# Rotary halves swapped by DMA instead of a second projection, and the second layer's gates on GpSimd

## The chip, the cores and the metric

One core of a Trainium2 chip runs one program. The time is device microseconds of the whole program, median of the runs. The engines named below are TensorE (PE: PE for matmuls, PEld for weight loads), VectorE (DVE), ScalarE (ACT), GpSimd (POOL) and SyncE (SP), which here only issues DMAs. Each engine runs its own instructions strictly in the order in which they are written and waits at semaphores, so an instruction that waits holds up everything behind it on its engine.

## What is computed

Two transformer layers over x of shape (8, 512, 128). What the change touches is the first attention, with 16 query heads and 4 key heads of 64, and the gates of the second attention. For each of them the reference says:

```python
def _rotate_half(t):
    t1, t2 = (t[..., :DH // 2], t[..., DH // 2:])
    return jnp.concatenate([-t2, t1], axis=-1)
...
q = q * cos + _rotate_half(q) * sin
k = k * cos + _rotate_half(k) * sin
...
attn = jax.nn.softmax(attn, axis=-1)
...
g = jax.nn.sigmoid(g.reshape(B, H, T, 2, 4).sum(-1))
gate_a = g[..., 0:1]
gate_b = g[..., 1:2]
gate_a_1 = gate_a * (gate_b * grep_a - 1.0) + 2.0
attn = attn + gate_a_1 * position_bias[None]
probs = jax.nn.softmax(attn, axis=-1)
```

The middle line on softmax belongs to the first attention, the last lines to the second one. After each attention comes a small feed-forward part, which the change leaves alone.

## The kernel before

**The first attention** works on 64 pairs of heads (8 sequences of 8 pairs), one pair to a *step*. The function `pipeline` writes the order of one step as eight *slots* by hand, and all engines walk through the same list, each taking its own part. Steps 3 to 50 are three rounds of a loop of 16 steps; the others are written out. In step s the list has:

- `C` (s, i), one in each slot: two 512-column matmuls give the scores of one key tile (L446, L448), ScalarE exponentiates them (L516), and `L` takes the rounding rest of the exponentials, on VectorE for two of the eight tiles (L607) and on GpSimd for six (L664).
- `D`: probabilities times values, eight blocks of twelve short matmuls (L464 to L466); VectorE normalises after each half (L613, L615). The first block of a half needs all `L` tiles of that half.
- `A` for pair s+3: the query projection, in three 512-column matmuls for q and three more for q with the halves of each head exchanged (L409 to L411; the exchanged weights are a copy made at the start, L559). VectorE multiplies both by cosine and sine in one pass into `rcs` (L585).
- `RS`, `RH`, `RL` for the same pair: GpSimd adds the two products (`rot`, L647), ScalarE rounds to 16 bits (`rhi`, L522), GpSimd takes the rest (`rlo`, L652). At `RL` SyncE waits for `rlo` and issues four DMAs that lay hi and lo parts out as query rows (L364, L366).
- `B` for pair s+2, four times: scores of the rounded parts for the row maximum (L431), reduced by VectorE (L600). `MX` and `M` turn the maxima, and SyncE sends them with one small DMA (L381) that `C` of the next step waits for.
- `O`: the transposes of a finished pair (L473, L538).

Once in eight steps come `W` (the output projection, L479, with L623 and L669), `HT` (transposes of the normalised input, L401), `K` twice (like `A`, for keys, with six DMAs each at `KL`, L375 to L377) and `V`. `A`, `K`, `B`, `M`, `O`, `V`, `HT` and `W` are *jobs*: each takes one of two PSUM buffers `ps_m`, which it can fill when the reader of the job before the last has freed it.

**The second attention** does its score products partly on VectorE and partly on GpSimd, in four rounds (`for r in range(QT)`). In a round VectorE makes the gates (L1440, L1443, L1446) with a drain behind each, then four products and eight sums, then the `residual` of the round before (L1431), which waits for TensorE, and only then the scores (L1464 to L1469); ScalarE exponentiates, and both engines multiply by the values (`p_prod`, L1477 and L1392). GpSimd multiplies the gates into the bias after its own score products (L1384). `statistics` and `spread` are the layer norm of a later round.

## Time and profile before

| what | value |
|---|---|
| median of 3 runs | 1565.05 us (1561.4 to 1566.12) |
| profiled execution, time | 1566.98 us |
| profiled execution, span of its instructions | 1565.2 us |
| first attention, first to last exponential | 93.9 to 863.7 us |
| second attention with its weights | about 1125 to 1337 us |
| TensorE busy, whole span | 1159.0 us |

A timeline row gives the start in us from the span's start, the duration in us, engine, line, operation, output and inputs, shape and count, and in square brackets how long the engine stood idle before it and who released it. A matmul's duration overlaps the next one's, so what one costs is read from the distance between starts.

### The profile page before, as it was taken

To read this page: it belongs to the slowest core of one execution; us is meant where nothing else is said; L and a number is where in the kernel's file an instruction comes from. 1 tells how busy PE (TensorE), PEld (TensorE's weight loads), DVE (VectorE), ACT (ScalarE), POOL (GpSimd) and SP (SyncE) were. 2 spreads that over 40 slices of the span, in tenths; PEclk is the share of its full clock that TensorE was granted. 3 is DMA by queue.
4 is the path that set the end of the run, shared out by engine and by line. 5 is a ranking of instruction groups with operands and counts; after the bars stand their busy time and mean duration, and the time that the engine had idled before them with its cause. 6 is when DMAs were issued, how large, how long until landed. Compare 5 with 4: busy or idle time off the path is not lost. (4 is left out here: it accounts for less than half of the span.)

```text
span 1565.2 us, 29826 instructions
## 1 busy us (share of the span) xinstructions
PE 1159.0 (74%) x10864; PEld 749.5 (48%) x10864; DVE 1129.2 (72%) x1571; ACT 608.1 (39%) x1176; POOL 835.0 (53%) x754
## 2 busy tenths in 40 slices
PE   2288999989999899999999446555358776165554
PEld 1135565646656556566666324434126566133343
DVE  2477978768788587787878368984339786568983
ACT  1135545445455364554546123332133330133331
POOL 0267879778788687887878123231035453023320
PEclk9589999999999999999999768987656788668986
DMA  2322113122132121311211000000000000000001
GB/s 65 87 45 59 39 32 66 43 49 51 33 66 43 29 60 32 66 43 37 61 34 31 15 0 1 1 0 0 24 1 1 1 0 1 14 1 0 1 0 54
DMA packets 52197, 46.37 MB, mean 30 GB/s; under 512 B 7734, under 2 KB 50250, under 8 KB 52042
## 3 DMA queue, kind: packets, MB, share of 16 engines
q1 hardware_dynamic: 52042, 44.33, 12.6%
q8 instruction: 94, 1.54, 0.4%
q14 instruction: 61, 0.50, 0.1%
HBM read 6.42 MB, written 2.10 MB: 5 GB/s over the span
## 5 line engine op out<-in xcount | busy, mean ns | idle before, releaser
L664 POOL TENSOR_TENSOR a_p_lo<-a_probs 128x512 f16<-128x512 f32 x384 | 419.8, 1115 | 26.2 <-ACT a_probs L516 22.7
L516 ACT ACTIVATE a_probs<-a_ps_s 128x512 f32<-128x512 f32 x512 | 303.6, 596 | 328.6 <-PE a_ps_s L448 321.1
L600 DVE TENSOR_REDUCE a_nmx<-a_ps_m 128x2 f32<-128x1024 f32 x256 | 311.1, 1216 | 39.3 <-PE a_ps_m L431 37.6
L464 PE MATMUL a_ps_o<-a_v_hi,a_probs 128*128 128x65 f16 x2048 | 238.7, 194 | 7.0 <-POOL a_p_lo L664 7.0
L466 PE MATMUL a_ps_o<-a_v_hi,a_p_lo 128*128 128x65 f16 x2048 | 238.0, 194 | 0.0
L465 PE MATMUL a_ps_o<-a_v_lo,a_probs 128*128 128x64 f16 x2048 | 237.8, 193 | 0.0
L464 PEld LDWEIGHTS a_ps_o<-a_v_hi,a_probs 128*128 128x128 bf16 x2048 | 191.5, 98 | 61.6 <-issue 14.6
L465 PEld LDWEIGHTS a_ps_o<-a_v_lo,a_probs 128*128 128x128 bf16 x2048 | 189.3, 98 | 44.1 <-issue 0.6
L446 PE MATMUL a_ps_s<-a_qq,a_kk 128*128 128x512 f16 x512 | 195.8, 382 | 10.6 <-issue 6.5
L448 PE MATMUL a_ps_s<-a_qq,a_k_l 65*128 65x512 f16 x512 | 196.7, 384 | 0.0
L825 PE MATMUL f_ps_gu<-f_w_gu,f_hqT 128*128 128x352 f32 x256 | 122.9, 643 | 90.5 <-DVE f_h L912 79.5
L466 PEld LDWEIGHTS a_ps_o<-a_v_hi,a_p_lo 128*128 128x128 f16 x2048 | 189.1, 97 | 0.0
L431 PE MATMUL a_ps_m<-a_kk,a_rhi 128*128 128x512 f16 x512 | 155.8, 386 | 16.4 <-DMA a_k_l<-a_rlo 9.5
L585 DVE TENSOR_TENSOR a_rcs<-a_ps_m,a_cossin 128x1024 f32<-128x1024 f32 x80 | 98.0, 1225 | 65.5 <-PE a_ps_m L411 64.7
L607 DVE TENSOR_TENSOR a_p_lo<-a_probs 128x512 f16<-128x512 f32 x128 | 143.2, 1119 | 1.7 <-ACT a_probs L516 1.7
L825 PEld LDWEIGHTS f_ps_gu<-f_w_gu,f_hqT 128*128 128x128 f32 x256 | 65.1, 267 | 140.2 <-issue 115.8
L647 POOL TENSOR_TENSOR a_rot<-a_rcs 128x512 f32<-128x512 f32 x80 | 107.8, 1347 | 45.3 <-DVE a_rcs L585 45.2
L652 POOL TENSOR_TENSOR a_rlo<-a_rot,a_rhi 128x512 f16<-128x512 f32 x80 | 92.6, 1157 | 40.1 <-ACT a_rhi L522 40.1
L998 POOL TENSOR_TENSOR f_q<-f_r,f_s 128x512 f32<-128x512 f32 x16 | 16.9, 1057 | 139.6 <-DVE f_r L932 139.6
L1287 PE MATMUL a_ps_o<-a_p_prod,ident 128*128 128x128 f32 x512 | 68.6, 304 | 28.7 <-DVE a_p_prod L1477 28.7
L431 PEld LDWEIGHTS a_ps_m<-a_kk,a_rhi 128*128 128x128 f16 x512 | 43.4, 99 | 93.0 <-DVE a_nmx L600 39.2
L848 PE MATMUL f_ps_y<-f_w_dn,f_h2T 128*128 128x128 f32 (+1 forms) x384 | 56.4, 301 | 36.4 <-ACT f_h2T L889 36.4
(217 smaller groups left out, 2123.5 us busy)
## 6 DMA issues: line engine op xcount, KB each, us to landing
a_qq<-a_rhi SPq DMA_DIRECT2D x128, 128.0 KB, 2.4
a_kk<-a_rhi SPq DMA_DIRECT2D x64, 128.0 KB, 2.4
a_qq<-a_rlo SPq DMA_DIRECT2D x128, 64.0 KB, 2.1
a_k_l<-a_rlo SPq DMA_DIRECT2D x32, 64.0 KB, 2.1
out_x<-x_sb SPq DMA_DIRECT2D x1, 2048.0 KB, 8.7
a_qq<-a_nmT SPq DMA_DIRECT2D x64, 2.0 KB
m_w<-in_wmod SPq DMA_DIRECT2D x2, 384.0 KB
a_probs<-in_wq SPq DMA_DIRECT2D x1, 512.0 KB, 3.5
```

Source lines behind the costliest of these rows:

```text
L431: last = nc.tensor.matmul(ps_m[:, n % 2, k, :], rhi[:, r % NR, qt * 128:(qt + 1) * 128], kk[:, b % 2, 2 * j // G0, 1 + h, :], start=True, ...
L446: nc.tensor.matmul(ps_s[:, i % 2, :], kk[:, b % 2, g, 0, kt * 128:(kt + 1) * 128], q_hl[:, p % 4, h, :], start=True, stop=False)
L448: nc.tensor.matmul(ps_s[:, i % 2, :], k_l1[:, b % 2, g, kt * 128:(kt + 1) * 128], q_hm[:, p % 4, h, :], start=False, stop=True).then_inc(s ...
L464: nc.tensor.matmul(out, hi, v_hi[:, b % 2, kt, g, 0:65], start=(kt == 0), stop=False)
L465: nc.tensor.matmul(out[:, 0:DH0], hi, v_lo[:, b % 2, kt, g, :], start=False, stop=False)
L466: last = nc.tensor.matmul(out, lo, v_hi[:, b % 2, kt, g, 0:65], start=False, stop=(kt == QT - 1))
L516: nc.scalar.activation(probs[:, p % 2, kt, h, :], ps_s[:, i % 2, :], ACT.Exp, scale=DH0 ** -0.5).then_inc(exp_done, 1)
L600: nc.vector.tensor_reduce(nmx[:, p % 2, 2 * i:2 * i + 2], ps_m[:, n % 2, :, :], axis=X, op=ALU.max, negate=True).then_inc(free[n % 2], 1)
L607: nc.vector.tensor_tensor(p_lo[:, p % 2, kt, h, :], pr, pr.bitcast(BF16)[:, 1:2 * L:2], ALU.subtract).then_inc(lo_dve, 1)
L647: nc.gpsimd.tensor_tensor(rot[:, r % 2, :], rcs[:, r % 2, 0, :], rcs[:, r % 2, 1, :], ALU.add).then_inc(rope_sum, 1)
L664: nc.gpsimd.tensor_tensor(p_lo[:, p % 2, kt, h, :], pr, pr.bitcast(BF16)[:, 1:2 * L:2], ALU.subtract).then_inc(lo_pool, 1)
L825: last = nc.tensor.matmul(ps_gu[:, t, a, 0:INNER], hqT[:, (2 * half + t) * 128:(2 * half + t + 1) * 128], w_gu[:, a * INNER:(a + 1) * INNE ...
```

## The change

In the first attention the second half of each projection goes: `A` and `K` are three matmuls into one bank, and the exchanged weights, their copies and a drain at the start go too. VectorE multiplies the one bank by cosine and by sine in the same single instruction (it reads the bank twice by a broadcast). The sine product is then moved by 32 partitions: a new item (`RD`, `KD`) on SyncE waits for VectorE and issues four DMAs of 32 partitions by 2 KB each into `rsw`, and the sum on GpSimd waits for these four. The slots are written anew: `A` comes first in its step, `B` in slots 1, 3, 5, 7, `O` in slot 2, and the sum, the rounding and the rest in slots 4, 5 and 6; for keys they reach into the next step. VectorE takes `L` tiles 3 and 7 instead of 2 and 6.

In the second attention the gates move to GpSimd, as four instructions with a drain behind each, behind its score products. On VectorE the residual of the round before now comes after the scores.

```diff
@@ pipeline
+        if pair(s + 3):
+            slots[0].append(("A", s + 3))
+            slots[1].append(("RD", s + 3))
+            slots[4].append(("RS", s + 3))
+            slots[5].append(("RH", s + 3))
+            slots[6].append(("RL", s + 3))
         if pair(s + 2):
             for i in range(4):
-                slots[2 * i].append(("B", s + 2, i))
-        if pair(s + 3):
-            slots[1].append(("A", s + 3))
-            slots[3].append(("RS", s + 3))
-            slots[4].append(("RH", s + 3))
-            slots[5].append(("RL", s + 3))
+                slots[2 * i + 1].append(("B", s + 2, i))
...
         if pair(s - 2):
-            slots[3].append(("O", s - 2))
+            slots[2].append(("O", s - 2))
...
         if (b := seq(-5)) is not None:
             for m in range(2):
-                slots[2 + 3 * m].append(("K", b, m))
-                slots[4 + 2 * m].append(("KS", b, m))
-                slots[5 + 2 * m].append(("KH", b, m))
-                slots[6 + m].append(("KL", b, m))
+                slots[2 + 2 * m].append(("K", b, m))
+                slots[3 + 2 * m].append(("KD", b, m))
+                slots[5 + 2 * m].append(("KS", b, m))
+            slots[6].append(("KH", b, 0))
+            slots[7].insert(0, ("KL", b, 0))
         if (b := seq(-4)) is not None:
+            slots[0].append(("KH", b, 1))
+            slots[1].append(("KL", b, 1))
...
-        LO_DVE, LO_POOL = (2, 6), (0, 1, 3, 4, 5, 7)
+        LO_DVE, LO_POOL = (3, 7), (0, 1, 2, 4, 5, 6)
@@ sync
+                if kind in ("RD", "KD"):
+                    key = it[1:]
+                    r = rope[key]
+                    t.jobs(free, job[("A" if kind == "RD" else "K",) + key], 1)
+                    for k in range(4):
+                        src, dst = slice(32 * k, 32 * (k + 1)), slice(32 * (k ^ 1), 32 * (k ^ 1) + 32)
+                        sp.dma_start(rsw[dst, r % 2, :], rcs[src, r % 2, 1, :]).then_inc(rope_swap[r % 2], 16)
@@ tensor
-                    for swap in range(2):
-                        out = ps_m[:, n % 2, swap, :]
-                        hi, lo = (w[:, swap, j * 128:(j + 1) * 128] for w in (w_hi, w_lo))
-                        nc.tensor.matmul(out, hi, hT_hi[:, b % 2, :], start=True, stop=False)
-                        nc.tensor.matmul(out, hi, hT_lo[:, b % 2, :], start=False, stop=False)
-                        last = nc.tensor.matmul(out, lo, hT_hi[:, b % 2, :], start=False, stop=True)
+                    hi, lo = (w[:, j * 128:(j + 1) * 128] for w in (w_hi, w_lo))
+                    nc.tensor.matmul(bank, hi, hT_hi[:, b % 2, :], start=True, stop=False)
+                    nc.tensor.matmul(bank, hi, hT_lo[:, b % 2, :], start=False, stop=False)
+                    last = nc.tensor.matmul(bank, lo, hT_hi[:, b % 2, :], start=False, stop=True)
@@ vector, before the loop
-            for w, heads in ((wq_hi, H0), (wq_lo, H0), (wk_hi, KV0), (wk_lo, KV0)):
-                w4 = w[:].rearrange("p s (h a c) -> p s h a c", h=heads, a=2)
-                for a in range(2):
-                    last = nc.vector.tensor_copy(w4[:, 1, :, a, :], w4[:, 0, :, 1 - a, :])
...
-                    nc.vector.tensor_tensor(rcs[:, r % 2, :, :], ps_m[:, n % 2, :, :], cossin[:],
+                    nc.vector.tensor_tensor(rcs[:, r % 2, :, :], ps_m[:, n % 2, 0:1, :].to_broadcast([128, 2, L]), cossin[:],
                                             ALU.mult).then_inc(free[n % 2], 1)
@@ gpsimd
-                    t.jobs(free, job[("A" if kind == "RS" else "K",) + key], 1)
+                    t.wait(rope_swap[r % 2], (r // 2 + 1) * 64, ROPE16 // 2 * 64)
                     t.ropes(rope_lo, r - 1, 1)
-                    nc.gpsimd.tensor_tensor(rot[:, r % 2, :], rcs[:, r % 2, 0, :], rcs[:, r % 2, 1, :],
+                    nc.gpsimd.tensor_tensor(rot[:, r % 2, :], rcs[:, r % 2, 0, :], rsw[:, r % 2, :],
                                             ALU.add).then_inc(rope_sum, 1)
@@ second attention, gpsimd
-                pool.wait_ge(gate_ok, r + 1)
+                pool.wait_ge(sig_ok, r + 1)
+                if r >= 1:
+                    pool.wait_ge(gbias_ok, r)
+                nc.gpsimd.tensor_tensor(gate[:], sig[:, r % 2, :, 1, :],
+                                        grep_a[:].unsqueeze(1).to_broadcast([128, B, H1]), ALU.mult)
+                nc.gpsimd.drain()
+                nc.gpsimd.tensor_tensor(gate[:], gate[:], gate_c[:, 0:1, :].to_broadcast([128, B, H1]), ALU.subtract)
+                nc.gpsimd.drain()
+                nc.gpsimd.tensor_tensor(gate[:], gate[:], sig[:, r % 2, :, 0, :], ALU.mult)
+                nc.gpsimd.drain()
+                nc.gpsimd.tensor_tensor(gate[:], gate[:], gate_c[:, 1:2, :].to_broadcast([128, B, H1]), ALU.add)
+                nc.gpsimd.drain()
+                if r >= 1:
+                    pool.wait_ge(score_ok, r)
@@ second attention, vector
-                dve.wait_ge(sig_ok, r + 1)
-                if r >= 1:
-                    dve.wait_ge(gbias_ok, r)
-                nc.vector.tensor_tensor(gate[:], sig[:, r % 2, :, 1, :],
...
-                nc.vector.tensor_scalar(gate[:], gate[:], 2.0, None, ALU.add).then_inc(gate_ok, 1)
...
-                if has(r - 1):
-                    residual(r - 1)
                 dve.wait_ge(gbias_ok, r + 1)
...
                                         ALU.subtract).then_inc(score_ok, 1)
+                if has(r - 1):
+                    residual(r - 1)
```

SyncE in one ordinary step inside the loop and at the start of the next, before. The first four rows are the query rows of one pair, `a_qq<-a_nmT` is the turned maxima:

```order
80 L364 DMA a_qq<-a_rhi 64x2x512 [waits a0_rlo]
81 L366 DMA a_qq<-a_rlo 64x512
82 L364 DMA a_qq<-a_rhi 64x2x512
83 L366 DMA a_qq<-a_rlo 64x512
84 L292 REGISTER_ALU
85 L381 DMA a_qq<-a_nmT 1x8x128 [waits a0_free0]
```

The same place after, from one pair's swap to the next pair's:

```order
163 L370 DMA a_rsw<-a_rcs 32x512 [waits a0_free1]
164 L370 DMA a_rsw<-a_rcs 32x512 x3
165 L298 REGISTER_ALU
166 L394 DMA a_qq<-a_nmT 1x8x128 [waits a0_free1]
167 L298 REGISTER_ALU
168 L377 DMA a_qq<-a_rhi 64x2x512 [waits a0_rlo]
169 L379 DMA a_qq<-a_rlo 64x512
170 L377 DMA a_qq<-a_rhi 64x2x512
171 L379 DMA a_qq<-a_rlo 64x512
172 L298 REGISTER_ALU
173 L370 DMA a_rsw<-a_rcs 32x512 [waits a0_free1]
174 L370 DMA a_rsw<-a_rcs 32x512 x3
```

Four swap DMAs now stand ahead of the maxima, and the next pair's swap stands behind the four query DMAs, which wait for `rlo`.

GpSimd in the step with the keys, after (two steps' worth of sums, `a_rot`, and rests, `a_rlo`):

```order
188 L652 TENSOR_TENSOR a_rot<-a_rcs,a_rsw 128x512 [waits a0_rlo,a0_rswap0]
189 L298 REGISTER_ALU
190 L669 TENSOR_TENSOR a_p_lo<-a_probs 128x512 [waits a0_edone]
191 L652 TENSOR_TENSOR a_rot<-a_rcs,a_rsw 128x512 [waits a0_rlo,a0_rswap1]
192 L298 REGISTER_ALU
193 L657 TENSOR_TENSOR a_rlo<-a_rot,a_rhi 128x512 [waits a0_rhi]
194 L298 REGISTER_ALU
195 L669 TENSOR_TENSOR a_p_lo<-a_probs 128x512 [waits a0_edone]
```

Each sum waits for a swap (`a0_rswap`), where before it waited for VectorE alone, and the query's `rlo` stands behind the first key's sum.

VectorE in the second attention, from the sums of a round to its scores, before (`a1_psum`, `a1_full` are TensorE's):

```order
897 L1450 TENSOR_TENSOR a_s_prod<-a_ps_q,a_qkvg 128x1024
898 L1414 TENSOR_REDUCE a_score<-a_s_prod 128x128 [waits a1_smd] x2
899 L1414 TENSOR_REDUCE a_score<-a_s_prod 128x128 [waits a1_smp] x4
900 L1431 TENSOR_TENSOR x_sb<-a_ps_r,x_sb 128x4x128 [waits a1_full0]
901 L1431 TENSOR_TENSOR x_sb<-a_ps_r,x_sb 128x4x128 [waits a1_full1]
902 L1464 TENSOR_TENSOR a_score<-a_score,a_gbias 128x1024 [waits a1_ssum,a1_gbias]
```

and after:

```order
885 L1461 TENSOR_TENSOR a_s_prod<-a_ps_q,a_qkvg 128x1024
886 L1435 TENSOR_REDUCE a_score<-a_s_prod 128x128 [waits a1_smd] x2
887 L1435 TENSOR_REDUCE a_score<-a_s_prod 128x128 [waits a1_smp] x4
888 L1473 TENSOR_TENSOR a_score<-a_score,a_gbias 128x1024 [waits a1_ssum,a1_gbias]
889 L1476 TENSOR_REDUCE a_mx<-a_score 128x128
890 L1478 TENSOR_TENSOR a_score<-a_score,a_mx 128x1024
891 L1452 TENSOR_TENSOR x_sb<-a_ps_r,x_sb 128x4x128 [waits a1_full0]
```

The residual's two instructions have moved from ahead of the scores to behind them.

## Rows read from the trace of the kernel before

**Rows 1.** The page's first part: busy time, share of the span, instructions.

```profile
PE 1159.0 (74%) x10864; PEld 749.5 (48%) x10864; DVE 1129.2 (72%) x1571; ACT 608.1 (39%) x1176; POOL 835.0 (53%) x754
```

**Rows 2.** Busy time in stretches: eight steps, W's step, K's and V's, an ordinary one.

```profile
core 0: us, PE busy (x) PEld busy (x) DVE busy (x) ACT busy (x) POOL busy (x), PEclk, DMA share, GB/s
408.62:506.09 97.47, 94.15 (x1142) 59.61 (x1142) 78.22 (x105) 51.53 (x102) 80.34 (x73) 1.00 0.23 48
408.62:428.42 19.80, 18.08 (x200) 13.80 (x200) 12.02 (x18) 7.37 (x14) 12.11 (x12) 1.00 0.12 25
428.42:454.75 26.33, 24.73 (x287) 14.93 (x286) 19.65 (x24) 14.02 (x27) 23.66 (x22) 1.00 0.38 82
475.36:485.60 10.24, 10.24 (x133) 6.12 (x132) 9.07 (x12) 6.03 (x13) 8.92 (x9) 1.00 0.20 42
```

**Rows 3.** Timeline of the ordinary step 475.36 to 485.60, all engines.

```profile
476.31 0.38 PE L409 MATMUL a_ps_m<-a_hT_hi,a_wq_hi 128*128 128x512 f16 x1
...
477.39 0.38 PE L411 MATMUL a_ps_m<-a_hT_hi,a_wq_lo 128*128 128x512 f16 x1
...
477.90 1.23 DVE L585 TENSOR_TENSOR a_rcs<-a_ps_m,a_cossin 128x1024 f32<-128x1024 f32 x1 [0.95 <-PE a_ps_m L411]
...
479.20 1.27 POOL L647 TENSOR_TENSOR a_rot<-a_rcs 128x512 f32<-128x512 f32 x1 [0.50 <-DVE a_rcs L585]
...
480.51 1.04 POOL L664 TENSOR_TENSOR a_p_lo<-a_probs 128x512 f16<-128x512 f32 x1
...
481.64 0.62 ACT L522 ACTIVATE a_rhi<-a_rot 128x512 f16<-128x512 f32 x1
...
482.33 1.16 POOL L652 TENSOR_TENSOR a_rlo<-a_rot,a_rhi 128x512 f16<-128x512 f32 x1 [0.79 <-ACT a_rhi L522]
...
483.52 0.63 SPq L364 DMA_DIRECT2D a_qq<-a_rhi  x1
...
485.48 1.66 SPq L366 DMA_DIRECT2D a_qq<-a_rlo  x1
```

**Rows 4.** The page's costliest groups: VectorE's cosine and sine product.

```profile
L585 DVE TENSOR_TENSOR a_rcs<-a_ps_m,a_cossin 128x1024 f32<-128x1024 f32 x80 | 98.0, 1225 | 65.5 <-PE a_ps_m L411 64.7
```

**Rows 5.** DMA issues: KB each, median us from issue to landing.

```profile
a_qq<-a_rlo SPq DMA_DIRECT2D x128, 64.0 KB, 2.1
...
a_b_hl<-a_b_lo SPq DMA_DIRECT2D x1, 0.8 KB, 1.7
```

**Rows 6.** Timeline of TensorE, 406 to 448 us: W, and HT behind its wait.

```profile
408.35 7.31 PE L479 MATMUL a_ps_m<-a_wo,a_oT 128*128 128x128 f32 x64
...
424.01 0.65 PE L401 MATMUL a_ps_m<-ident,a_xhat 128*128 128x128 f32 x4 [1.50 <-DVE a_nmx L600]
```

**Rows 7.** Timeline of the start: first sum, first B; below, the first exponential.

```profile
63.88 1.27 POOL L647 TENSOR_TENSOR a_rot<-a_rcs 128x512 f32<-128x512 f32 x1 [4.14 <-DVE a_rcs L585]
...
76.53 1.01 PE L431 MATMUL a_ps_m<-a_kk,a_rhi 128*128 128x512 f16 x2 [9.45 <-DMA a_k_l<-a_rlo]
...
93.88 0.60 ACT L516 ACTIVATE a_probs<-a_ps_s 128x512 f32<-128x512 f32 x1 [3.01 <-PE a_ps_s L448]
```

**Rows 8.** Timeline of the second attention, round 1, all engines.

```profile
1201.60 1.49 DVE L1440 TENSOR_TENSOR a_gate<-a_sig,a_grep_a 128x128 f32<-128x128 f32 x1
...
1207.29 2.34 DVE L1450 TENSOR_TENSOR a_s_prod<-a_ps_q,a_qkvg 128x1024 f32<-128x1024 f32 x2
...
1214.21 2.34 POOL L1384 TENSOR_TENSOR a_gbias<-a_gate,a_bias 128x1024 f32<-128x1024 f32 x1
...
1228.91 0.69 DVE L1431 TENSOR_TENSOR x_sb<-a_ps_r,x_sb 128x512 f32<-128x512 f32 x1 [6.88 <-PE a_ps_r L1268]
...
1230.92 1.22 DVE L1464 TENSOR_TENSOR a_score<-a_score,a_gbias 128x1024 f32<-128x1024 f32 x1
...
1235.41 0.60 ACT L1351 ACTIVATE a_ps_p<-a_score 128x512 f32<-128x512 f32 x1 [4.18 <-DVE a_score L1469]
...
1237.56 4.58 DVE L1477 TENSOR_TENSOR a_p_prod<-a_ps_p,a_qkvg 128x1024 f32<-128x1024 f32 x4
```

More of the change, by code:

```diff
@@ L236, in layer0_attention @@
         rcs = sb("rcs", [128, 2, 2, L])
+        rsw = sb("rsw", [128, 2, L])
         rot = sb("rot", [128, 2, L])
@@ L488, in _ @@
             nc.scalar.activation(ident16[:], ident[:], ACT.Copy).then_inc(ready, 1)
-            for whole, hi in ((wq, wq_hi[:, 0, :]), (wk, wk_hi[:, 0, :]), (wv, wv_hi[:])):
+            for whole, hi in ((wq, wq_hi[:]), (wk, wk_hi[:]), (wv, wv_hi[:])):
                 nc.scalar.activation(hi, whole, ACT.Copy, scale=WSCALE).then_inc(w_hi_done, 1)
@@ L550, in _ @@
             dve.wait_ge(w_hi_done, 3)
-            for whole, hi, lo in ((wq, wq_hi[:, 0, :], wq_lo[:, 0, :]), (wk, wk_hi[:, 0, :], wk_lo[:, 0, :]),
-                                  (wv, wv_hi[:], wv_lo[:])):
-                nc.vector.scalar_tensor_tensor(out=lo, in0=whole, scalar=WSCALE, in1=hi, op0=ALU.mult,
-                                               op1=ALU.subtract)
-            nc.vector.drain()
-            for w, heads in ((wq_hi, H0), (wq_lo, H0), (wk_hi, KV0), (wk_lo, KV0)):
-                w4 = w[:].rearrange("p s (h a c) -> p s h a c", h=heads, a=2)
-                for a in range(2):
-                    last = nc.vector.tensor_copy(w4[:, 1, :, a, :], w4[:, 0, :, 1 - a, :])
-            last.then_inc(swapped, 1)
+            for whole, hi, lo in ((wq, wq_hi[:], wq_lo[:]), (wk, wk_hi[:], wk_lo[:]), (wv, wv_hi[:], wv_lo[:])):
+                last = nc.vector.scalar_tensor_tensor(out=lo, in0=whole, scalar=WSCALE, in1=hi, op0=ALU.mult,
+                                                      op1=ALU.subtract)
+            last.then_inc(split, 1)
             def item(t, it):
```

31 lines of the change are left out of this document (15 added, 16 removed).

## Prediction

> **What bounds the kernel now.** The busy shares of the whole span say little: TensorE is at 74% and VectorE at 72% [rows 1], averages over stages with different limits. So the first attention, half of the span, is read by its steps. A cycle of eight steps (one sequence) takes 97.47 us [rows 2]. An ordinary step takes 10.24 us and TensorE is busy for all of it, with 9.07 for VectorE and 8.92 for GpSimd [rows 2]. A busy TensorE need not be a full one, but in the timeline its matmuls of that step stand start to start with no idle bracket [rows 3]: it sets the 10.24. Two places are different. W's step takes 19.80, of which W is 7.31 and a wait of HT for VectorE's reduction 1.50 [rows 2, 6]. The step with K and the one with V take 26.33 together, 23.66 of it GpSimd's [rows 2]. In the second attention VectorE paces each round: it works on gates from 1201.60 to 1207.29, later stands idle for 6.88 us at the residual, and only then makes the scores that ScalarE waits 4.18 us for [rows 8].
>
> **What leaves TensorE.** Six projection matmuls start at 476.31 to 477.39, so one costs 1.08 / 5 = 0.216 us [rows 3]. Three go in each of 80 ropes [rows 4]: 0.65 us a step, 80 x 0.65 = 52 us in all. An ordinary step would need 10.24 - 0.65 = 9.59 us of TensorE. VectorE's product keeps its one pass of 1.23 us over as many elements; a broadcast read is not in the trace, I take it at the same price (if it cost twice, VectorE's 9.07 would rise to 10.3 and the gain would be gone). Its wait of 0.95 us for the projection [rows 3] only shrinks.
>
> **What takes its place on SyncE.** This decides the forecast. Before, the sum followed VectorE's product at once: `rot` starts at 479.20, right after the product of 477.90 + 1.23 [rows 3]. Now SyncE issues four DMAs first. Behind them on SyncE's queue stand the maxima and then the four query DMAs, and these wait for `rlo`, which comes out of this very swap; the next pair's swap stands behind them. So one turn around SyncE, DMA, GpSimd and SyncE can't overlap with the next one. Its length, from rows:
> - first to fourth swap issue: query DMAs go at 483.52 and, three issues later, 485.48, so 0.65 apiece: 1.96;
> - landing of the fourth: 2.1, as for the 64 KB `rlo` rows [rows 5]; between 1.7 (the 0.8 KB row) and 2.4 as the outer ends;
> - `rot` 1.27, the `p_lo` tile between it and `rlo` 1.04, `rlo` 1.16 [rows 3] (ScalarE's `rhi`, 0.62, hides beside the tile);
> - four query issues 2.6, and 0.2 for five handovers of some 0.04.
>
> Sum 1.96 + 2.1 + 3.47 + 2.6 + 0.2 = 10.3 us. That is more than TensorE's 9.59 and hardly less or more than today's 10.24: **SyncE's turn replaces TensorE as the bound, and an ordinary step keeps its time.** Some issues take longer, like the 1.66 at 485.48 [rows 3]; before they hid, now eight of eight stand in the turn. I take 10.55 a step, with 10.0 and 11.3 as ends (short landing; one long issue in each turn). The first two steps after V can borrow about 1 us, since a swap may lag behind its product by that much before TensorE feels it.
>
> **The eight-step cycle.** (a) W's 7.3 us give SyncE's turn all the slack it needs, so its step and the one before it cost TensorE's work: 30.04 before; after 2 x 9.59 + 7.31 + 0.44 for HT's transposes = 26.9. HT's 1.50 goes, since in the new order HT waits for a reduction two jobs back that is done by then. -2.9 with 0.2 of small waits. (b) K's and V's steps. I followed the queues from K's step's projection at 0: product ends 2.1, swap issued to 4.8, landed 6.3, `rot` to 7.5; the first key's product ends about 6.4 (behind the first reduction on VectorE), its swap lands 10.5, and GpSimd holds `rlo` of the query behind that sum: `rlo` 13.0. Then SyncE issues without a gap: 4 query DMAs to 15.6, 6 key DMAs to 19.6, the next swap to 22.2, 6 key DMAs to 26.1, and only then the maxima, landed 28. The scores of V's successor wait for those, so the pair of steps takes 28.5, against 26.33: +2.2, with long issues +2.6. TensorE would need some 22. (c) The other four steps: 9.6 + 10.2 + 2 x 10.55 = 40.9 against 41.1. Sum of a cycle: -2.9 + 2.6 - 0.2 = -0.5 us; seven cycles carry ropes: **-4 us** (ends: -35 and +30).
>
> **The start.** Eight weight copies and three matmuls ahead of the first product go, 1.3 us each. Then the first sum (63.88) waits for a swap, 1.96 + 2.1 + 0.4; the second key's and the first query's swap queue behind the first's and behind twelve key DMAs, so the first B (76.53) comes about 6 us later, and the first scores wait for maxima that stand behind one more swap: the first exponential (93.88) about 7.5 us later [rows 7]. **+7.5 us.**
>
> **The second attention.** Gates off VectorE: 1207.29 - 1201.60 = 5.7 us a round. GpSimd's four gate operations are 128 wide: its 1024-wide one takes 2.34 [rows 8], an eighth is 0.3, with a drain 0.45, so four take about 2 us; VectorE's own small ones took up to 2.2 each there, and four of those, 9 us, are the upper end. They stand behind GpSimd's score products, which end at 1214.2 [rows 8], and the scores need the bias from about 1221: 7 us of cover less 2.34. So they cost nothing at the lower price, and about 4 us a round at the upper one in the first round, less later, when GpSimd starts earlier.
> The residual is on the round's cycle: TensorE's sums, its turn through ScalarE, residual, then the 4.5 us of scores (1230.92 to the exponential at 1235.41) and the exponential, then `p_prod` at 1237.56. With scores first, they run inside the 6.88 us of idle time, and `p_prod` follows residual and statistics at once. What is late next is ScalarE (sigmoid and two table loads until about 1231). Round 1: -4.5 for the scores and -3 carried from round 0, whose GpSimd products no longer wait for `spread`; round 2 another -4; round 3 another -1, since there the residual hid almost entirely. **-12 us** (ends -6 and -13).
> Beside this, the rule of the Trainium skill, *GPSIMD Engine Reference*, Engine selection, that elementwise work with two inputs is about twice as slow on GpSimd as on VectorE, speaks against moving gates: at twice VectorE's undisturbed 0.7 us they would be 6 us, still within the cover of all rounds but the first.
>
> **Sum.** 1566.98 (the profiled execution) - 4 + 7.5 - 12 = 1558.5; it lay 1.9 us above the median, so **1556.5 us**.
>
> **Rivals.**
> *The turn is shorter than TensorE's step.* Landing at 1.7 and an issue of 0.5 would give 9.3. Then the 52 us come, less what GpSimd's lag costs (swap data reach it 6 us after the projection, and the next block of D waits for tiles behind it: about 9.75 a step). Cycle: 5 x -0.5, -2.4 for W's step, -2 for K and V: -7, seven times -49 with the start at +5 and -12: 1508; half of it 1530. Against it: every SBUF to SBUF issue in the rows takes 0.6 or more.
> *The turn is longer, and the kernel slower.* Place: SyncE's queue between the query DMAs and the next swap. The forecast's -8.5 is used up when an ordinary turn takes 0.25 us more than 10.55 (35 such steps), so from 10.8. With a long issue in each turn, or ScalarE's `rhi` stuck behind an exponential as in the 0.79 us wait before `rlo` [rows 3], it is 11.3: 35 x 0.75 = 26 more, and some 6 in K's and V's steps: 1588.
> *Gates late on GpSimd.* The upper price eats most of the second attention's gain: 1565.
> *The swap's form.* The Trainium skill, *DMA: Bandwidth & Descriptors*, Rules for kernel authors, says that transfers to disjoint partition parts serialise and should be one. Here the rows give the cost: 1.96 us of the turn are the three extra issues. By that rule one DMA would make the turn 8.4 us; the change has four, so it stays a reason for the bound, not a time of its own.
> That the change doesn't do what it says is out: TensorE's list has three matmuls a projection.
>
> **Chances.** SyncE's turn at 10.3 to 10.7 as forecast: 0.43 (mostly faster, partly the same); shorter turn 0.15; longer turn 0.24; late gates 0.10; the rest 0.08. A measurement of this kernel can tell about 0.3% from no change, 4.7 us. Faster 0.32 + 0.15 + 0.02 + 0.04 = 0.53; same 0.19; slower 0.28. The range of 1525 to 1590 leaves out the full gain and the far end of the longer turn.
>
> **What would show it.** SyncE's queue without idle time between the query DMAs and the next swap, and each swap issued later after its product than 0.1 us; `rot` waiting on a swap in most steps, with ordinary steps at 10.3 to 10.7 and TensorE idle about 0.7 us in them; the first exponential at 101; K's and V's steps near 28.5, W's near 17.5; in the second attention no idle time before the residual ahead of the scores, and `p_prod` of round 3 12 us earlier against the stage's start. I am wrong if ordinary steps fall below 10, if swaps land in more than 2.4 us, or if the broadcast product takes more than 1.23.

## The result, and the profile after

| kernel | time, median | span of the profiled execution |
|---|---|---|
| before | 1565.59 us (1561.4 to 1567.8) | 1565.2 us |
| after | 1595.8 us (1593.12 to 1596.28) | 1591.3 us |

The change makes the kernel slower: ratio 1.0193, interval 1.0168 to 1.0217. The forecast was 1556.5, with 1525 to 1590 as its range; the time lies outside it, on the side of the rival with the longer turn.

First the page of after: TensorE's, VectorE's and GpSimd's busy time in all, then VectorE's product, GpSimd's sum and ScalarE's rounding of the rotated rows, and the swap's DMAs (KB each, median us to landing).

```profile
PE 1127.5 (71%) x10624; PEld 734.6 (46%) x10624; DVE 1079.7 (68%) x1551; ACT 599.5 (38%) x1176; POOL 832.9 (52%) x772
...
L652 POOL TENSOR_TENSOR a_rot<-a_rcs,a_rsw 128x512 f32<-128x512 f32 x80 | 104.3, 1304 | 149.2 <-DMA a_rsw<-a_rcs 149.1
...
L590 DVE TENSOR_TENSOR a_rcs<-a_ps_m,a_cossin 128x1024 f32<-128x1024 f32 x80 | 97.9, 1224 | 77.5 <-PE a_ps_m L422 72.4
...
L533 ACT ACTIVATE a_rhi<-a_rot 128x512 f16<-128x512 f32 x80 | 50.4, 630 | 157.0 <-POOL a_rot L652 157.0
...
a_rsw<-a_rcs SPq DMA_DIRECT2D x320, 64.0 KB, 2.0
```

TensorE is busy 31.5 us less than in [rows 1], and the kernel takes longer all the same. 240 matmuls are gone, as forecast, but they give 31.5 us and not 52. That fits the clock: the granted clock stood at its lower level for 462 us of this span and for 412 before, and the same work takes longer there. 512-column matmuls stand 0.43 us apart at 60.0 us, at the lower level, and 0.22 apart at 63.5, at the upper one. The prices of the parts are as forecast: the product over a broadcast takes 1224 ns (1225 in [rows 4]), a swap lands 2.0 us after its issue. But GpSimd stands idle 149 us for the swap, and ScalarE 157 us behind GpSimd, where it had been 46 before.

Where the time went is seen in stretches whose ends are first exponentials of pairs: of before, seven cycles; of after, the same seven, then one cycle, W's step, the steps of K and V, and an ordinary step (columns as in [rows 2]).

```profile
93.88:783.54 689.66, 657.39 (x7837) 410.10 (x7836) 548.21 (x723) 359.46 (x706) 560.46 (x503) 0.99 0.22 48
```

```profile
102.04:822.95 720.91, 631.59 (x7626) 400.07 (x7625) 525.37 (x722) 351.72 (x707) 551.99 (x502) 0.97 0.32 71
433.02:536.42 103.40, 90.50 (x1112) 58.06 (x1112) 76.19 (x105) 50.48 (x101) 78.94 (x73) 0.98 0.32 71
433.02:451.27 18.25, 17.75 (x197) 13.47 (x197) 11.60 (x17) 7.14 (x14) 12.03 (x13) 1.00 0.17 38
451.27:482.21 30.94, 22.87 (x276) 13.78 (x275) 21.60 (x26) 13.66 (x28) 24.85 (x23) 1.00 0.49 107
502.83:513.98 11.15, 9.66 (x130) 5.95 (x129) 8.61 (x12) 5.91 (x12) 8.56 (x8) 1.00 0.27 61
```

The seven cycles take 31.25 us more (720.91 - 689.66). With the start's 8.2 (102.04 for 93.88), the second attention's -11.1 (below) and -2.2 of small differences elsewhere, that is the 26.1 us between the two spans. In an ordinary step TensorE works 9.66 us, as forecast, but the step takes 11.15 here and 10.65 on average.

The turn itself, in the timeline of after, from one pair's swap to the next one's:

```profile
415.63 2.47 SPq L370 DMA_DIRECT2D a_rsw<-a_rcs  x4
...
418.67 0.69 SPq L394 DMA_DIRECT2D a_qq<-a_nmT  x1
...
419.61 1.27 POOL L652 TENSOR_TENSOR a_rot<-a_rcs,a_rsw 128x512 f32<-128x512 f32 x1 [1.51 <-DMA a_rsw<-a_rcs]
...
420.84 1.04 POOL L669 TENSOR_TENSOR a_p_lo<-a_probs 128x512 f16<-128x512 f32 x1
...
420.91 0.63 ACT L533 ACTIVATE a_rhi<-a_rot 128x512 f16<-128x512 f32 x1 [1.43 <-POOL a_rot L652]
...
421.84 1.16 POOL L657 TENSOR_TENSOR a_rlo<-a_rot,a_rhi 128x512 f16<-128x512 f32 x1
...
423.02 0.68 SPq L377 DMA_DIRECT2D a_qq<-a_rhi  x1
...
425.04 0.61 SPq L379 DMA_DIRECT2D a_qq<-a_rlo  x1
425.76 2.47 SPq L370 DMA_DIRECT2D a_rsw<-a_rcs  x4
```

From 415.63 to 425.76 it is 10.13 us, link by link the forecast's chain of 10.3, and SyncE goes from the last query DMA to the next swap without a pause. At the start, with softmax not yet running, the same ring is bare: the sums stand 9.8 and 10.2 us apart, and the first scores wait 3.03 us for the maxima.

```profile
80.20 1.26 POOL L652 TENSOR_TENSOR a_rot<-a_rcs,a_rsw 128x512 f32<-128x512 f32 x1 [8.79 <-DMA a_rsw<-a_rcs]
...
90.02 1.26 POOL L652 TENSOR_TENSOR a_rot<-a_rcs,a_rsw 128x512 f32<-128x512 f32 x1 [6.67 <-DMA a_rsw<-a_rcs]
...
100.21 1.26 POOL L652 TENSOR_TENSOR a_rot<-a_rcs,a_rsw 128x512 f32<-128x512 f32 x1 [7.04 <-DMA a_rsw<-a_rcs]
```

The second attention, round 1, timeline of after, which answers to [rows 8]:

```profile
1250.45 0.49 POOL L1394 TENSOR_TENSOR a_gate<-a_sig,a_grep_a 128x128 f32<-128x128 f32 x1
...
1252.87 2.34 POOL L1405 TENSOR_TENSOR a_gbias<-a_gate,a_bias 128x1024 f32<-128x1024 f32 x1
...
1261.23 1.23 DVE L1473 TENSOR_TENSOR a_score<-a_score,a_gbias 128x1024 f32<-128x1024 f32 x1
...
1265.88 0.69 DVE L1452 TENSOR_TENSOR x_sb<-a_ps_r,x_sb 128x512 f32<-128x512 f32 x1 [0.19 <-PE a_ps_r L1274]
...
1268.22 0.60 ACT L1357 ACTIVATE a_ps_p<-a_score 128x512 f32<-128x512 f32 x1
...
1270.17 2.32 DVE L1488 TENSOR_TENSOR a_p_prod<-a_ps_p,a_qkvg 128x1024 f32<-128x1024 f32 x2
```

The four gate operations take 2.4 us on GpSimd (1250.45 to 1252.87), the bias is ready long before the scores, and the residual's idle time has shrunk from 6.88 to 0.19 us. From the stage's first sigmoid to its last product with the values (`p_prod`, round 3) it is 144.4 us before and 133.3 after: 11.1 less.

### The profile page after: what moved, and what is told of

Same layout as the page of the kernel before. It is cut to its first block and busy times, and to the rows that moved or that the text cites. A ratio compares the mean times of both kernels' runs of the same rounds, so it can differ in the third digit from the quotient of the medians.

```text
span 1591.3 us, 29726 instructions
## 1 busy us (share of the span) xinstructions
PE 1127.5 (71%) x10624; PEld 734.6 (46%) x10624; DVE 1079.7 (68%) x1551; ACT 599.5 (38%) x1176; POOL 832.9 (52%) x772
## 5 line engine op out<-in xcount | busy, mean ns | idle before, releaser
L527 ACT ACTIVATE a_probs<-a_ps_s 128x512 f32<-128x512 f32 x512 | 297.5, 595 | 275.2 <-PE a_ps_s L459 271.5
L475 PE MATMUL a_ps_o<-a_v_hi,a_probs 128*128 128x65 f16 x2048 | 243.1, 196 | 11.3 <-POOL a_p_lo L669 9.7
L477 PE MATMUL a_ps_o<-a_v_hi,a_p_lo 128*128 128x65 f16 x2048 | 242.4, 195 | 0.0
L476 PE MATMUL a_ps_o<-a_v_lo,a_probs 128*128 128x64 f16 x2048 | 242.2, 194 | 0.0
L652 POOL TENSOR_TENSOR a_rot<-a_rcs,a_rsw 128x512 f32<-128x512 f32 x80 | 104.3, 1304 | 149.2 <-DMA a_rsw<-a_rcs 149.1
L442 PE MATMUL a_ps_m<-a_kk,a_rhi 128*128 128x512 f16 x512 | 160.8, 398 | 16.9 <-ACT a_rhi L533 12.1
L590 DVE TENSOR_TENSOR a_rcs<-a_ps_m,a_cossin 128x1024 f32<-128x1024 f32 x80 | 97.9, 1224 | 77.5 <-PE a_ps_m L422 72.4
L612 DVE TENSOR_TENSOR a_p_lo<-a_probs 128x512 f16<-128x512 f32 x128 | 105.8, 826 | 5.7 <-ACT a_probs L527 5.7
L533 ACT ACTIVATE a_rhi<-a_rot 128x512 f16<-128x512 f32 x80 | 50.4, 630 | 157.0 <-POOL a_rot L652 157.0
L442 PEld LDWEIGHTS a_ps_m<-a_kk,a_rhi 128*128 128x128 f16 x512 | 47.6, 101 | 95.7 <-DVE a_nmx L605 27.3
L457 PEld LDWEIGHTS a_ps_s<-a_qq,a_kk 128*128 128x128 f16 x512 | 50.4, 99 | 81.5 <-ACT a_probs L527 45.7
```

Of the source, the lines that this page charges most:

```text
L442: last = nc.tensor.matmul(ps_m[:, n % 2, k, :], rhi[:, r % NR, qt * 128:(qt + 1) * 128], kk[:, b % 2, 2 * j // G0, 1 + h, :], start=True, ...
L457: nc.tensor.matmul(ps_s[:, i % 2, :], kk[:, b % 2, g, 0, kt * 128:(kt + 1) * 128], q_hl[:, p % 4, h, :], start=True, stop=False)
L475: nc.tensor.matmul(out, hi, v_hi[:, b % 2, kt, g, 0:65], start=(kt == 0), stop=False)
L476: nc.tensor.matmul(out[:, 0:DH0], hi, v_lo[:, b % 2, kt, g, :], start=False, stop=False)
L477: last = nc.tensor.matmul(out, lo, v_hi[:, b % 2, kt, g, 0:65], start=False, stop=(kt == QT - 1))
L527: nc.scalar.activation(probs[:, p % 2, kt, h, :], ps_s[:, i % 2, :], ACT.Exp, scale=DH0 ** -0.5).then_inc(exp_done, 1)
```

## Experiments

Times are medians, ratios are to before with their intervals. "Seven cycles" is the stretch that took 689.66 us before and 720.91 after. The first theory is the forecast's: **SyncE's turn** holds the step, since a swap stands behind DMAs that wait for the swap before. Its rivals: the latency of the swap in the order of GpSimd's and ScalarE's queues, or the new order of instructions as such.

### What the swap costs, and what the rest

Without the swap (the exchange left out):

```diff
-                if kind in ("RD", "KD"):
+                if kind in ("none",):
...
-                    nc.gpsimd.tensor_tensor(rot[:, r % 2, :], rcs[:, r % 2, 0, :], rsw[:, r % 2, :],
+                    nc.gpsimd.tensor_tensor(rot[:, r % 2, :], rcs[:, r % 2, 0, :], rcs[:, r % 2, 1, :],
```

> The changed kernel without the swap's DMAs: GpSimd adds VectorE's unexchanged sine product instead, so the exchange of the halves is left out of the computation and so is SyncE's part of the turn; all else, the new order of the instructions too, stays. Both T and R put the loss in the swap: T expects about what the opened ring gives or some us less, 1535 to 1555 us, with ordinary steps of 9.6 to 9.8; R expects the same here but not in the run with the late query DMAs. A third theory N (the new order of instructions in the step, not the swap, costs the time: swapped places of B and A, key sums later, other tiles on VectorE) expects 1580 us or more.

Measured: 1504.58 us, ratio 0.9612 (0.9594 to 0.9631), seven cycles 652.03 us. The theory that the new order of instructions costs the time is out; without the swap the kernel is 91 us faster than with it. This is also the price list of the idea: the rest of the change is worth 61 us, the swap takes 91. In the seven cycles 37.6 us of TensorE's 45.5 (70 x 0.65) are gained; what takes the other 8 is not shown, and the new order can have a part in it.

The second layer's part alone, put on the kernel before:

> The kernel before with only the second attention of the changed kernel (gates on GpSimd, residual behind the scores). The prediction's step for it: 12 us less, 6 to 13, so 1553 to 1559 us; the traces of before and after put it at 11 to 13. If the second attention gained only because of its later start or other surroundings in the changed kernel, the gain here differs from 11 by more than 2 us.

Measured: 1551.53 us, ratio 0.9914 (0.9897 to 0.9932), 13 us less than before. That step of the forecast (-12) stands.

### How many DMAs the swap is

One DMA of 128 rows (a copy, without the exchange):

```diff
-                    for k in range(4):
-                        src, dst = slice(32 * k, 32 * (k + 1)), slice(32 * (k ^ 1), 32 * (k ^ 1) + 32)
-                        sp.dma_start(rsw[dst, r % 2, :], rcs[src, r % 2, 1, :]).then_inc(rope_swap[r % 2], 16)
+                    sp.dma_start(rsw[:, r % 2, :], rcs[:, r % 2, 1, :]).then_inc(rope_swap[r % 2], 16)
```

> The changed kernel with one DMA of 128 partitions per swap in place of four of 32; it copies the sine product without exchanging the halves, so the exchange is left out of the computation, but the swap's place and its bytes are the same. It takes three issues of about 0.65 us out of the turn, 1.96 us. T: the turn falls from 10.65 to about 8.7 us, below TensorE's 9.6, so an ordinary step takes 9.6 to 9.9 and the kernel 1550 to 1565 us. R (latency, not SyncE's time): the landing keeps its 2 us, less than 8 us are gained from the earlier end of the last part, 1586 to 1597; if the one larger DMA lands later than 2.5 us, T loses part of its gain as well.

Measured: 1523.41 us, ratio 0.9731 (0.9701 to 0.9762), seven cycles 657.58 us. Three issues less give back 72 us, more than was expected; the page's row for the swap:

```profile
a_rsw<-a_rcs SPq DMA_DIRECT2D x80, 256.0 KB, 2.3
```

So four times the bytes land 0.3 us later than a 64 KB part, but go out as one issue. To tell the count from the shape, the same bytes as four uneven parts:

```diff
+                    for rows in (slice(0, 1), slice(1, 2), slice(2, 3), slice(3, 128)):
+                        sp.dma_start(rsw[rows, r % 2, :], rcs[rows, r % 2, 1, :]).then_inc(rope_swap[r % 2], 16)
```

> The unexchanged copy again (the exchange of the halves is left out of the computation), the same bytes, but as four DMAs: 1, 1, 1 and then 125 partitions. T2 and T3 (the number of issues on SyncE is what costs): the three small ones bring back 1.9 us per swap and with them nearly all of the loss, 1580 to 1600 us against 1523 with one DMA. Theory L (the shape and the bytes of the four parts cost, or their packets' contention): the small ones are free, 1520 to 1540.

Measured: 1739.86 us, ratio 1.1129 (1.1099 to 1.116), far above both expectations. SyncE and GpSimd in the timeline of this kernel:

```profile
509.23 2.66 SPq L369 DMA_DIRECT2D a_rsw<-a_rcs  x4
...
515.94 1.27 POOL L651 TENSOR_TENSOR a_rot<-a_rcs,a_rsw 128x512 f32<-128x512 f32 x1 [2.69 <-DMA a_rsw<-a_rcs]
```

The last issue ends at 511.89 and the sum can start at 515.94, 4.05 us later; in after these are 418.10 and 419.61, 1.51 us. A DMA of 125 partitions is slow to land, so this run told nothing of the count. Again with 16, 16, 16 and 80 partitions:

> The unexchanged copy of the swap (the exchange of the halves is left out of the computation), the same bytes as in the run with one DMA, as four DMAs of 16, 16, 16 and 80 partitions on SyncE. Issue count theory: the turn is as long as in the changed kernel (four issues of 0.6 us, the last part landing in 2.0 to 2.4), 1580 to 1605 us against 1523 with one DMA. Shape theory (four DMAs of 32 rows cost for something else than their number): 1520 to 1550.

Measured: 1611.44 us, ratio 1.0291 (1.0267 to 1.0316), seven cycles 739.1 us; its parts land in 2.0 and 2.4 us. Four issues bring the loss back although three of them are small, a little more than in after and than was expected. The number of issues costs.

### Opening SyncE's ring without touching the swap

Query DMAs a step later, behind the next swap; key DMAs later too:

```diff
+        if pair(s + 2):
+            slots[2].append(("RQ", s + 2))
...
+            slots[5].append(("KQ", b, 0))
+        if (b := seq(-3)) is not None:
+            slots[5].append(("KQ", b, 1))
...
-                elif kind == "RL":
+                elif kind == "RQ":
```

> The changed kernel with one edit: on SyncE alone, the four DMAs that carry a pair's rotated queries stand one step later, behind the next pair's swap, and the key DMAs half a step to a step later, behind the maxima's DMA. No other engine's order changes. Theory T (SyncE's turn: the next swap stands behind DMAs that wait for this pair's rlo, which waits for this pair's swap): the ring is open, an ordinary step goes from 10.65 us back to TensorE's 9.6 to 9.9, the K and V steps together from 31 to 27 to 28, and the kernel takes 1545 to 1560 us. Rival R (the swap's latency of 2 us itself, which GpSimd and ScalarE wait out in the order of their queues with softmax tiles behind it, sets the step; SyncE's order does not matter): less than 6 us are gained, 1588 to 1597.

Measured: 1589.93 us, ratio 1.0162 (1.0136 to 1.0189). By its expectation this was the rival's number. So I took up the rival in a sharper form: ScalarE rounds the sum ahead of three exponentials, and its wait there would be a second ring. Two runs move that rounding two exponentials later, the first without the late DMAs, the second with them:

```diff
+            if seq(-5) is None:
+                slots[7].append(("RH", s + 3))
...
+        if pair(s + 2) and seq(-4) is None:
+            slots[0].append(("RL", s + 2))
```

> The changed kernel with one edit: in steps without keys ScalarE rounds the rotated rows to fp16 (rhi) two exponentials later, at the step's end, and GpSimd's rlo follows at the start of the next. SyncE's DMAs stay behind rlo and ahead of the next swap. T2: this lengthens SyncE's ring (rlo comes about 2 us later, q DMAs and the next swap with it), so it is slower than the changed kernel: ordinary steps 11.5 to 12.5, 1620 to 1680 us. A theory A in which only ScalarE's wait for the sum holds the step expects a gain, 1550 to 1575 us.

> The same later rhi and rlo, and the query and key DMAs a step later on SyncE: both rings are opened, with the swap still four DMAs. T2: neither edit alone helps (late DMAs alone took 1590), both together do: ordinary steps 9.6 to 9.9, 1545 to 1565 us with the K and V steps as they are. If the four DMAs cost for another reason (contention of their packets with GpSimd or the queue), it stays at 1580 or above.

Measured: 1689.4 us, ratio 1.0765 (1.0718 to 1.0812), and 1590.18 us, ratio 1.0145 (1.0113 to 1.0178). The first is a little beyond what SyncE's ring had given (a later `rlo` lengthens the turn: seven cycles 807.95 us) and far from the rival. The second misses. Its timeline shows why:

```profile
608.23 3.51 SPq L380 DMA_DIRECT2D a_rsw<-a_rcs  x4
611.85 0.67 SPq L387 DMA_DIRECT2D a_qq<-a_rhi  x1
...
614.57 0.71 SPq L404 DMA_DIRECT2D a_qq<-a_nmT  x1
```

```profile
616.42 0.39 PE L467 MATMUL a_ps_s<-a_qq,a_kk 128*128 128x512 f16 x1 [1.06 <-DMA a_qq<-a_nmT]
```

My own edit had made a new ring: the late query DMAs stood ahead of the maxima, which TensorE's next scores need. The waits of the kernel with the late DMAs alone over the first attention (us, times, longest) say the same of it, and that its keys came too late as well:

```profile
PE a_ps_m L447 <- DMA a_k_l<-a_rlo: 16.4, 7, 2.5
PE a_ps_s L462 <- DMA a_qq<-a_nmT: 10.9, 14, 1.6
```

So the query DMAs were put behind the maxima (slot 5 for slot 2), the keys left alone:

> The changed kernel, four-part swap, with the four query DMAs one step later on SyncE, but this time behind the maxima's DMA of that step, not ahead of it; key DMAs unchanged. The trace of the run with late rhi and late DMAs showed a third ring that the edit itself had made: TensorE's first scores waited for the maxima's row, which stood behind the late query DMAs (swap 2.5, four issues 2.6, maxima 0.7 and its landing). Theory T3 (three rings of nearly one length: SyncE's through rlo, ScalarE's wait for the sum, the maxima behind late DMAs): with the first and the third open and the second closed, ordinary steps 10.0 to 10.5 and 1575 to 1592 us. If SyncE's ring was the only one in the changed kernel, 9.6 to 9.9 and 1550 to 1565.

Measured: 1547.99 us, ratio 0.9886 (0.9869 to 0.9902), seven cycles 692.49 us, first exponential at 95.19. 48 us come back by moving four DMAs past the maxima and the next swap, with nothing else changed; this is faster than before. The two profiles put 28.4 us into the seven cycles and 6.9 into the start. And with ScalarE's rounding late as well:

> The same, and rhi two exponentials later with rlo behind it, so that ScalarE's ring is open too. T3: ordinary steps at TensorE's 9.6 to 9.8 with the swap still four DMAs, K and V steps about as in the changed kernel (30 to 31 together), 1545 to 1565 us. If it stays above 1580, the four DMAs cost in a way that none of the three rings holds.

Measured: 1553.94 us, ratio 0.9918 (0.9901 to 0.9934). No gain: ScalarE's wait in ordinary steps bounds nothing. The expectation of a second ring falls. With SyncE's ring open the five steps from the one behind V to the one before W take 9.85 us on average, 9.58 without any swap; no other ring of weight is left there.

### The steps of K and V

With that ring open, K's and V's steps still took 30.6 us on average over the seven cycles (30.9 in after, 26.9 before). Next the key DMAs went past the next swap, and the second keys' behind the maxima (`KQ`, 0 in slot 2 and `KQ`, 1 in slot 5 of V's step):

> The changed kernel with its query DMAs behind the maxima and one step later (1548 us), and now the key DMAs too, not a full step but past the next swap: the first keys' six behind it, ahead of the maxima, the second keys' six last in that step. If the K and V steps are long because a pair's swap and the maxima stand behind twelve key DMAs that wait for rlo: K and V together 27.5 to 28.5 for 30.6 and 1527 to 1537 us. If GpSimd's and ScalarE's own order (the sum of the second keys, for which ScalarE waited 4.4 us) is what costs there: 30 us and more, 1543 to 1552.

Measured: 1545.49 us, ratio 0.9875 (0.9838 to 0.9912): 29.2 us for the two steps, but no gain in the whole that the intervals can tell. GpSimd and ScalarE there:

```profile
543.98 1.60 POOL L660 TENSOR_TENSOR a_rlo<-a_rot,a_rhi 128x512 f16<-128x512 f32 x1
...
546.54 1.26 POOL L655 TENSOR_TENSOR a_rot<-a_rcs,a_rsw 128x512 f32<-128x512 f32 x1
```

```profile
547.92 0.63 ACT L536 ACTIVATE a_rhi<-a_rot 128x512 f16<-128x512 f32 x1 [4.37 <-POOL a_rot L655]
```

ScalarE waits 4.37 us for the second keys' sum, with exponentials behind it. So that rounding went two slots later, and the query DMAs behind the second keys' swap:

```diff
-            slots[0].append(("KH", b, 1))
-            slots[1].append(("KL", b, 1))
+            slots[2].append(("KH", b, 1))
+            slots[3].append(("KL", b, 1))
```

> The changed kernel's four-part swap with both moves: query and key DMAs behind the next swap, the second keys' rounding two exponentials later. If these were the causes of the long K and V steps: together 26.5 to 28 for 31 in the changed kernel, 1520 to 1535 us. If not: 1540 to 1550, as with the key DMAs moved alone (1545).

Measured: 1541.12 us, ratio 0.984 (0.9819 to 0.9861), 27.1 us for the two steps, but the step behind them went from 10.4 to 11.6. Less than expected, though outside the interval of the run with the query DMAs alone. K and V thus have more than one cause. Taken with the step behind them, since time is passed on to it, they take 37.3 us before, 41.1 in after, 39.7 with the DMAs moved on SyncE and 38.7 with the rounding late as well: 1.4 us for the DMAs' place, 0.9 for ScalarE's and GpSimd's order together with the last move of the query DMAs, and 1.5 that neither gives back. Without the swap it is 35.9. Where the last kernel stands is seen in one of its V steps, in which GpSimd is busy from end to end (10.13 of 10.57 us in the same step of before):

```profile
536.87:550.36 13.49, 10.25 (x125) 6.45 (x125) 8.35 (x12) 7.34 (x16) 13.49 (x13) 1.00 0.58 125
```

TensorE's clock is a second difference between the two kernels, so the 0.9 isn't all shown to be the order's: see the end.

### A version that beats both

A swap can be two DMAs if each rotated dimension lies next to its partner: even rows to odd ones and odd to even. Queries, keys and tables get the same order, so the products stay.

```diff
-                    for k in range(4):
-                        src, dst = slice(32 * k, 32 * (k + 1)), slice(32 * (k ^ 1), 32 * (k ^ 1) + 32)
-                        sp.dma_start(rsw[dst, r % 2, :], rcs[src, r % 2, 1, :]).then_inc(rope_swap[r % 2], 16)
+                    for k in range(2):
+                        sp.dma_start(rsw[1 - k:128:2, r % 2, :], rcs[k:128:2, r % 2, 1, :]
+                                     ).then_inc(rope_swap[r % 2], 16)
...
+        def beside(w):
+            w = w.rearrange("p (h c a) -> p a h c", a=2, c=DH0 // 2)
+            return [w[:, a, :, :] for a in range(2)]
```

> The changed kernel with the two halves of a head laid side by side (each rotated dimension next to its partner, in the weights' splits and the tables; queries and keys alike, so the products are the same), so that a swap is two DMAs of 64 partitions, even rows to odd and odd to even, 128 KB each, in place of four of 32. It does the exchange. Theory T2 (the number of issues sets the turn; two rings hold it at about 10.4 us, SyncE's and one through ScalarE's queue, which waits for GpSimd's sum ahead of the next exponentials): two issues of 0.65 leave both rings, 1.3 us, so they fall from 10.65 to 9.3 to 9.4, just below TensorE's 9.6: ordinary steps 9.6 to 9.9 and 1525 to 1545 us. Theory L (the one large DMA was faster for its shape, 128 partitions in one descriptor block, not for the count): most of the loss stays, 1570 to 1596 us. If the rows at a step of two partitions land later than 2.5 us, 1545 to 1570.

Measured: 1527.81 us, ratio 0.9747 (0.9717 to 0.9777); its parts of 128 KB land in 2.1 us. With the late DMAs of the run that made the third ring it took 1531.4 us (0.9734 to 0.9811), no different. With the query DMAs behind the maxima:

> The two-DMA swap (the candidate for the best version) with the query DMAs one step later behind the maxima; key DMAs unchanged. T3: its ordinary steps stand at 9.6 to 9.8 already, with single ones of 10.0 to 10.6 where an issue took over 1 us; the later DMAs take those away and shorten the K steps a little: 0 to 10 us below 1528. Above 1532 would say that the maxima or the keys are made later by it.

Measured: 1518.36 us, ratio 0.9706 (0.9686 to 0.9727). With the key DMAs moved 1516.11 us (0.9662 to 0.9726), with the query DMAs behind the second keys' swap 1512.72 us (0.9632 to 0.9674), and with the late rounding of the second keys:

> The same, and ScalarE rounds the second keys two exponentials later, with GpSimd's rlo two slots later. If ScalarE's wait in its queue ahead of the exponentials costs: 2 to 3 us less per pair of K and V steps, 1495 to 1510 us. If the wait only filled time in which TensorE was the bound anyway: within 4 us of the run with the query DMAs moved.

Measured: **1510.93 us, ratio 0.9644 (0.9616 to 0.9672)**, 3.6% below before and 5.3% below after; the last three can't be told from their neighbours, but the last two are outside the interval of the 1518 us. The last step gave 1.8 us, the smaller of its two expected outcomes: with two DMAs ScalarE's wait costs little or nothing. The best one's seven cycles, and its steps of K and V:

```profile
92.51:746.42 653.91, 614.87 (x7627) 390.78 (x7626) 538.66 (x723) 355.90 (x706) 568.01 (x503) 0.99 0.31 78
411.89:436.36 24.47, 22.24 (x274) 13.53 (x272) 19.55 (x26) 13.78 (x28) 24.03 (x21) 1.00 0.40 102
```

That is within 2 us of the kernel without any swap (652.03), whose order is that of after: in the cycles the swap is hidden. Of the 6 us between the two kernels the start holds the most, 92.51 for 87.02.

## Why the prediction was wrong

**What bounds the kernel, TensorE's work in a step, the price of the product: right.** TensorE's 9.66 us in an ordinary step is the forecast's 9.59.

**SyncE's turn: right in its mechanism and nearly in size.** 10.13 us without long issues against 10.3, 10.65 on average over the five steps from the one behind V to the one before W against 10.55. Moving the query DMAs alone took 48 us off, which shows it. The long issues are there: a swap of four that took 3.69 us at 442.08, for 2.47. The turn isn't closed in every step: in the seven cycles 38 of 63 swaps go out within 0.15 us of SyncE's DMA before them. The others go out later, most of them right behind VectorE's product, as in the step behind V in all seven cycles.

**The cycle of eight: the step that failed.** The forecast summed it to -0.5 us; measured, as the mean of seven, it is 103.0 - 98.5 = +4.5 (31.25 / 7). Its parts, from the distances between the first exponentials of the steps:

| part | before | after | forecast | measured |
|---|---|---|---|---|
| (a) the step before W, and W | 30.52 | 29.68 | -2.9 | -0.8 |
| (b) K's and V's steps | 26.88 | 30.86 | +2.6 | +4.0 |
| (c) the other four | 41.13 | 42.45 | -0.2 | +1.3 |

The turn itself was sized well, but the sum gave it to two ordinary steps of five only and put the other three at 9.59, 9.6 and 10.2; the "longer turn" rival counted 35 such steps, five a cycle. Of the 5.0 us a cycle by which the sum missed, the five ordinary steps are 2.7 (19 us in seven cycles), K's and V's steps 1.4 (10 us) and W's own step 0.9 (6 us).

In (a) the slack that W gives the turn was credited to the step before W too, where it isn't yet there: that step took 10.79, the turn's time, not 9.59. W's own step took 18.9, for 17.3; without the swap it is 18.9 as well, so this part isn't the swap's, and its cause stays open.

In (c) the two steps said to borrow from V took 10.25 and 10.48. The swap of the first wasn't held by SyncE (it goes out 0.03 us behind its product), so its 0.65 us over the forecast are not the turn's. This step took 11.74 and 11.05 us in the two cycles in which the granted clock was 0.88 and 0.85 there, and 9.5 to 10.5 in the other five, at 1.00. The second stands at the turn again in most cycles.

In (b) the chain on SyncE was followed rightly and came out too short. One K step and V step of after, on SyncE and ScalarE, from 451.27:

```profile
451.80 0.67 SPq L377 DMA_DIRECT2D a_qq<-a_rhi  x1
...
455.67 5.26 SPq L370 DMA_DIRECT2D a_rsw<-a_rcs  x8
...
465.01 0.68 SPq L377 DMA_DIRECT2D a_qq<-a_rhi  x1
...
469.72 0.63 ACT L533 ACTIVATE a_rhi<-a_rot 128x512 f16<-128x512 f32 x1 [4.38 <-POOL a_rot L652]
...
472.02 2.48 SPq L370 DMA_DIRECT2D a_rsw<-a_rcs  x4
...
479.52 0.71 SPq L394 DMA_DIRECT2D a_qq<-a_nmT  x1
...
482.21 0.60 ACT L527 ACTIVATE a_probs<-a_ps_s 128x512 f32<-128x512 f32 x1 [2.43 <-PE a_ps_s L459]
```

The first swap starts 4.4 us into the step and not at 2.2, behind the query DMAs of the pair before; the query DMAs start at 13.7 for 13.0; from there SyncE has no pause over 0.15 us, two of its issues take 0.95 and 1.48, and the maxima are issued at 28.3, where they were to have landed by 28. What the forecast did not follow is ScalarE's own queue, which waits 4.38 us for the second keys' sum with exponentials behind it. It is the next thing that holds these steps once the key DMAs are out of the way, together with GpSimd's work in V's step. The "longer turn" rival named the place rightly, and its price from 10.8 us per turn was the right warning. It put 26 us into the ordinary steps and 6 into K's and V's; 19 and 10 came, and W's 6.

**The start:** +8.2 for +7.5, by the same ring as forecast. **The second attention:** -11.1 in the profile and -13 alone, for -12. Its late-gates rival is out: four gate operations took 2.4 us, for the 2 forecast. The rule of the Trainium skill, *GPSIMD Engine Reference*, Engine selection, on two-input work at half VectorE's speed does not show at this size: the first gate product, of 128 columns, took 0.45 to 0.49 us on GpSimd, and 0.64 to 1.56 on VectorE before (what made it longer than 0.64 there is not shown). At 1024 columns the trace agrees with it: 2.34 us for the bias on GpSimd, 1.23 for the scores on VectorE.

**The swap's form** was in the forecast only as a reason for the bound, by the Trainium skill, *DMA: Bandwidth & Descriptors*, Rules for kernel authors. The runs agree with that rule: with one DMA, which copies and does not exchange, 1523 us for 1596. It deserved to be read as the change's main risk, since the three extra issues alone decided the sign: with two DMAs, which do exchange, 1528.

**The sum** in the end: 1566.98 + 8.2 + 31.25 - 11.1 - 2.2 = 1593.1, the profiled execution. The miss of 35 us in it is the cycle's: 7 x 5.

## What to carry to other kernels

When a transfer takes a computation's place, draw the ring that its issuing queue closes: what stands between this transfer and the next one of its kind, and which of that waits for this transfer's own result. If something does, move those waiting issues behind the next transfer, and then look at what now stands behind them, here the maxima. Count issues before bytes: one to two DMAs in place of four were worth 70 us here, while a DMA of four times the bytes landed 0.3 us later. Whether the same four DMAs cost less from another engine's queue was not tested.

A forecast of a cycle must give a bound to every step in which it holds, and a step is excused from it only by slack that is there before that step, not behind it. And it must follow each in-order queue through its crowded steps, not only the one that bounds the ordinary ones.
